# Softmax normalised after the value product, in the sparse attention of a macaron block

## The chip, the core and the metric

The kernel runs on one core of a Trainium2 chip as one program: feed-forward half, sparse attention, feed-forward half. The metric is the device time of one execution in microseconds. The engines are PE (matrix product; PEld is its weight load), DVE (vector), ACT (scalar and activation), POOL (GpSimd) and SP (which here only issues DMAs). Each runs its own instructions in program order and waits on semaphores for the others.

## What is computed

The input is 2 sequences of 1024 tokens of width 128. The change lies in the middle part, where every token attends to 96 keys:

```
_, idx = top_k(I, 96)                      # 64 newest keys, and the 32 best of the older ones
key_c = (c_kv @ W_uk)[bi, idx];  value = (c_kv @ W_uv)[bi, idx]
scores = (q_c . key_c + q_r . key_r) * scale        # 8 heads, content and rotary part
attn = softmax(scores, axis=-1)
out = einsum('bhlk,bhlkd->bhld', attn, value) ... @ W_out
```

The kernel keeps keys and values in the compressed form `c_kv` (32 numbers per token): the scores are taken against `c_kv` and the rotary part, the weights are applied to `c_kv`, and the products with `W_uv` and `W_out` are folded into one matrix used at the end.

## The kernel before

The two feed-forward halves take the first and the last third of the span and are not touched. The attention loop runs over 128 blocks (`NB`) of 16 tokens; a block has 128 rows (4 groups of 4 tokens and 8 heads, so 32 rows per group). Blocks come in 8 phases of 16, and within a phase two "far" and two "near" blocks alternate (`place`). For a block's 16 tokens there are 64-key windows that are local (`KL` for scores; `KVS` or `KV64`, a copy of it shifted by 64 tokens, for values) and 32 selected keys per token.

- A far block's selected rows are gathered by POOL, 4 indirect DMAs a block (line 620), from `kv_rows`, a table in HBM with 128 numbers per token: 64 rotary, 32 of `c_kv`, and 32 ones (`ROWG`; `ROWKV` is the first 96). PE transposes them (line 1001).
- A near block's selected rows come through one-hot matrices: POOL compares the list of indices with key numbers (line 639, 1 to 4 instructions a block, `chunks`), and PE multiplies the one-hot matrices with a table (line 1007). The indices reach POOL's partitions by a store to HBM and a broadcast load on SP (lines 501 and 507), once a phase; the load waits for DVE's last selection step of the phase ahead and for all of the current phase's one-hot matrices.

Per block x the engines then do:

- DVE turns the keys from PSUM with the rotary table into `GTS` (`dve_keys`, 1689); PE forms scores (`pe_scored`, 1020 to 1026); DVE takes the minimum (`dve_least`, 1698); ACT takes the exponential and its row sum `total` (`act_exp`, 1284, followed by a read of the accumulator); DVE takes 1/total (`dve_inverse`, 1703); ACT multiplies the block by it (`act_scaled`, 1290).
- PE transposes the 256 weights of each row (`pe_turned`, 1035), and for near blocks the values too (1038); ACT copies these from PSUM (`act_turned`, 1277); PE applies the weights to the values (`pe_mixed`, 1051 and 1054) and writes 32 rows x 128 columns of bank 7. Four blocks fill 32 rows x 512 columns, and DVE copies them to `OA` (`dve_attended`, two instructions of 256 columns, 1713). Bank 7 holds four such strips.
- Between these, DVE carries out the selection for the phases ahead (`dve_select`, 1647 to 1682) at block numbers fixed by a table, PE its products (982), ACT their relu (1255).

The order is written out by hand. On PE a loop step i is `pe_turned(i)`, `pe_keys(i+3)`, `pe_scored(i+2)`, index products, `pe_mixed(i)`; on DVE it is `dve_inverse(i+1)`, `dve_keys(i+3)`, `dve_least(i+2)`, on every fourth step `dve_attended`, then selection steps. `pe_keys` first calls `pe_stream`, which multiplies an identity by a mask into the bank that the keys will overwrite: 8 matmuls of 512 bf16 columns ahead of a phase's first block, 2 ahead of other far blocks (line 988), 176 in all. Nothing reads their results. After the loop SP moves `OA` to `OAX` by DMA (515) and PE multiplies by the folded matrix (951).

## Time and profile before

| | before |
|---|---|
| median of 3 runs (lowest to highest) | 2060.25 us (2053.6 to 2062.78) |
| the profiled execution | 2060.25 us |
| its span, first to last instruction | 2058.4 us |
| busy over the span: PE, DVE, ACT, POOL | 84%, 62%, 54%, 27% |
| mean granted PE clock over the span; from 790 to 1430 us | 0.849; 0.77 |
| attention loop | about 783 to 1433 us |

The span is the stretch from the first instruction to the last. A busy share is a mean over parts with different limits: POOL is 27% busy over the span and 67% (431.22 of 643 us) from 790 to 1433 us. The granted clock is PE's clock as a share of 2.4 GHz; it takes the values 1.00 and 0.50 (1.2 GHz). "Idle before, releaser" tells how long an engine stood still before an instruction and whose semaphore let it go on.

### The profile page before, as it was taken

To read this page: it belongs to the slowest core of one execution; us is meant where nothing else is said; L and a number is where in the kernel's file an instruction comes from. 1 tells how busy PE (TensorE), PEld (TensorE's weight loads), DVE (VectorE), ACT (ScalarE), POOL (GpSimd) and SP (SyncE) were. 2 spreads that over 40 slices of the span, in tenths; PEclk is the share of its full clock that TensorE was granted. 3 is DMA by queue.
4 is the path that set the end of the run, shared out by engine and by line. 5 is a ranking of instruction groups with operands and counts; after the bars stand their busy time and mean duration, and the time that the engine had idled before them with its cause. 6 is when DMAs were issued, how large, how long until landed. Compare 5 with 4: busy or idle time off the path is not lost.

```text
span 2058.4 us, 34052 instructions
## 1 busy us (share of the span) xinstructions
PE 1719.7 (84%) x10764; PEld 991.9 (48%) x10764; DVE 1285.0 (62%) x3053; ACT 1111.2 (54%) x2328; POOL 548.9 (27%) x479
## 2 busy tenths in 40 slices
PE   3899999699957457888888988888489999969995
PEld 1344444477744114445544545555334444447774
DVE  5677775577785565364655554533467777557777
ACT  3367777388845333333433334333236767738884
POOL 6000000000000505686667866663500000000000
PEclk9699999699987568876967778578769999969998
DMA  4111110111102251111121011120211111002110
GB/s 134 62 50 50 47 46 10 41 67 68 52 10 81 61 119 40 41 32 46 30 62 50 27 43 35 37 61 22 91 62 49 50 49 44 9 29 86 61 52 21
DMA packets 66505, 104.28 MB, mean 51 GB/s; under 512 B 19432, under 2 KB 37296, under 8 KB 63280
## 3 DMA queue, kind: packets, MB, share of 16 engines
q1 hardware_dynamic: 56720, 84.86, 12.9%
q0 software_dynamic: 8192, 16.79, 2.8%
q8 instruction: 73, 1.20, 0.2%
q10 hardware_dynamic: 1456, 0.90, 0.2%
q14 instruction: 64, 0.52, 0.1%
HBM read 74.80 MB, written 8.59 MB: 41 GB/s over the span
## 4 chain that ended last, share of the span: by engine, by line
PE 58%; POOL 11%; issue 10%; DVE 9%; ACT 5%; SPq 3%; DVEq 3%; DMA 1%; ACTq 0%; another core or an unknown queue 0%; POOLq 0%
PE bank L701 10%; PE bank L847 8%; PE bank L685 7%; PE bank L660 6%; PE bank L837 6%; POOL onehot L639 6%; POOL arena L620 5%; PE bank L1007 2%; ACT experts L1152 1%; PE bank L662 1%; PE bank L687 1%; PE bank L1020 1%; DVE arena L1319 1%; SPq L547 1%; PE bank L988 1%
## 5 line engine op out<-in xcount | busy, mean ns | idle before, releaser
L1319 DVE TENSOR_REDUCE arena<-bank 128x1 f32<-128x512 f32 (+3 forms) x768 | 383.1, 551 | 171.4 <-PE bank L662 117.5
L1079 ACT ACTIVATE arena<-bank 128x512 f32<-128x512 f32 (+3 forms) x768 | 335.5, 493 | 145.2 <-PE bank L687 122.2
L566 POOL TENSOR_TENSOR rstd<-vareps,neghalf 128x8 f32<-128x8 f32 x14 | 23.6, 1684 | 1165.3 <-DVE vareps L1312 1165.3
L660 PE MATMUL bank<-arena 72*128 72x512 bf16 (+3 forms) x768 | 259.9, 347 | 39.2 <-DMA arena<-arena 37.1
L620 POOL DMA_INDIRECT arena<-kv_rows,IDX x256 | 251.4, 982 | 153.2 <-ACT IDX L1248 83.9
L685 PE MATMUL bank<-arena 99*128 99x512 bf16 (+3 forms) x768 | 254.7, 335 | 6.1 <-ACT arena L1085 4.3
L639 POOL TENSOR_SCALAR onehot<-XT,const 128x512 fp32r<-128x512 f16 x136 | 212.5, 1574 | 167.3 <-DMA XT<-idx_rows 81.6
L701 PE MATMUL bank<-arena 128*32 128x512 f32 (+3 forms) x1536 | 225.8, 502 | 0.0
L1689 DVE TENSOR_TENSOR HN<-bank,RT 96x512 f32<-96x512 f32 x128 | 87.4, 683 | 218.0 <-PE bank L1007 136.6
L1377 DVE TENSOR_TENSOR experts<-arena,experts 128x512 fp32r<-128x512 f32 x256 | 171.5, 689 | 71.3 <-ACT experts L1152 71.3
L1284 ACT ACTIVATE ATT<-bank,col 128x256 f32<-128x256 f32 x128 | 60.7, 474 | 281.2 <-DVE col L1698 242.9
L1150 ACT ACTIVATE arena<-bank,bias 128x512 f32<-128x512 f32 x256 | 186.0, 727 | 45.8 <-PE bank L837 45.8
L837 PE MATMUL bank<-experts,experts 128*128 128x512 f32 x768 | 196.8, 403 | 7.4 <-ACT experts L1152 5.4
L1152 ACT ACTIVATE experts<-bank,bias 128x512 fp32r<-128x512 f32 x256 | 187.3, 732 | 0.0
L847 PE MATMUL bank<-experts,experts 128*128 128x512 f32 x768 | 182.2, 389 | 0.0
L685 PEld LDWEIGHTS bank<-arena 99*128 99x128 bf16 x768 | 75.5, 98 | 204.9 <-ACT arena L1079 141.0
L1007 PE MATMUL bank<-onehot,tab 128*96 128x512 f32 x272 | 111.2, 523 | 73.2 <-POOL onehot L639 72.3
L837 PEld LDWEIGHTS bank<-experts,experts 128*128 128x128 f32 x768 | 143.7, 192 | 54.7 <-ACT experts L1152 22.3
L847 PEld LDWEIGHTS bank<-experts,experts 128*128 128x128 f32 x768 | 144.1, 188 | 30.4
L660 PEld LDWEIGHTS bank<-arena 72*128 72x128 bf16 x768 | 77.8, 101 | 110.3 <-DVE arena L1319 44.5
L662 PE MATMUL bank<-mask_qk_b,ident_b 128*128 128x128 bf16 x512 | 117.3, 230 | 0.0
L687 PE MATMUL bank<-mask_kq_b,ident_b 128*128 128x128 bf16 x512 | 113.2, 222 | 0.0
(249 smaller groups left out, 2601.7 us busy)
## 6 DMA issues: line engine op xcount, KB each, us to landing
arena<-wt_rows SPq DMA_DIRECT2D x16, 1024.0 KB, 4.7
arena<-q_rows SPq DMA_DIRECT2D x192, 48.0 KB
arena<-k_rows SPq DMA_DIRECT2D x192, 48.0 KB
arena<-in_L_ffn_w SPq DMA_DIRECT2D x32, 256.0 KB, 5.0
arena<-arena SPq DMA_DIRECT2D x32, 256.0 KB
XT<-idx_rows SPq DMA_DIRECT2D x8, 1024.0 KB, 4.7
arena<-kv_rows,IDX POOLq DMA_INDIRECT x256
arena<-HN SPq DMA_DIRECT2D x32, 128.0 KB, 2.4
```

The source lines that it names most:

```text
L620: pool.indirect_dma_start(G[d % GR][:, g, :], None, kv_rows, bass.IndirectOffsetOnAxis(ap=IDX[:, q, k * GB + g:k * GB + g + 1], axis=0))\
L639: pool.tensor_scalar(OH[n % OHR][:, :], IDXB[:, k * BANK:(k + 1) * BANK], cst("key")[:, c:c + 1], None, ALU.is_equal)\
L660: m = pe.matmul(o[:, 0:hi - lo], QB[buf][s][0:ROWS, qt * P:(qt + 1) * P], KB[buf][s][0:ROWS, lo:hi], start=True, stop=True)
L685: m = pe.matmul(o[:, 0:hi - lo], KB[buf][s][0:rows, kc * P:(kc + 1) * P], QB[buf][s][0:rows, lo:hi], start=True, stop=True)
L701: m = pe.matmul(bank[6][r:r + STRIP, lo - hf * BANK:BANK], VS[buf][:, s, kc, :], PT[w % PT_RING][:, 0:(hf + 1) * BANK - lo], start=(kc == ...
L837: m = pe.matmul(bank[f][:, :], W1R[buf][w][:, f * P:(f + 1) * P], XR[x][:, tb * BANK:(tb + 1) * BANK], start=((w, x) == pairs[0]), stop=(( ...
L847: m = pe.matmul(bank[4 + k][:, :], W2R[buf][w][:, f, :], H1R[k][x][:, f, :], start=(f == 0 and (w, x) == pairs[0]), stop=(f == FC - 1 and ...
L1079: act.activation(PT[w % PT_RING][:, 0:m], bank[S_RING + w % S_RING][:, 0:m], ACT.Exp, scale=float(HD) ** -0.5)\
L1150: act.activation(H1[tb % 2][:, f, :], bank[f][:, :], ACT.Gelu_apprx_tanh, bias=bias1[buf][:, f:f + 1])
L1152: act.activation(H1R[tb % 2][0][:, f, :], bank[f][:, :], ACT.Gelu_apprx_tanh, bias=bias1[buf][:, f:f + 1]).then_inc(gelu_done, 1)
L1319: dve.tensor_reduce(rowmax[:, hf, s, qt:qt + 1], bank[u % S_RING][:, 0:n], AX_X, ALU.max).then_inc(max_done, 1)
L1377: dve.tensor_tensor(H1R[tb % 2][1][:, f, :], H1[tb % 2][:, f, :], H1R[tb % 2][0][:, f, :].bitcast(F32), ALU.subtract)\
```

## The change

The row sum is no longer taken by ACT, and the weights are no longer scaled before they are transposed. The block of 32 ones beside `c_kv` is carried along through all steps, so that the value product gives 64 rows: 32 of unnormalised output and 32 that each hold the sum of the weights. After four blocks DVE takes the reciprocal of the 32 x 512 sums and multiplies the output by it while it moves it to `OA`. For this:

- `dve_inverse`, `act_scaled`, the accumulator of `act_exp`, and `pe_stream` with its 176 matmuls go.
- Keys go through PE and DVE with 128 rows in place of 96 (free sizes stay); near values are 64 columns wide per group in place of 32, so ACT's near copy is 512 columns in place of 384; `KV64` is twice as wide, and its six DMAs with it.
- `PB` (weights before the transpose) has 2 buffers in place of 3; bank 7 holds 2 strips in place of 4, so the first value product of group j waits for `dve_attended(j-2)` in place of `(j-4)`.

The declarations of the two semaphores that go are left out here.

```diff
@@ -260,8 +260,6 @@
         col = sb("col", [P, 3])
-        total = sb("total", [P, 3])
-        inverse = sb("inverse", [P, 3])
         best = sb("best", [P, NSEL])
@@ -324,7 +322,7 @@
         KVS = view("sel", (NT, ROWG))
-        KV64 = view("sel", (NT, DC))
+        KV64 = view("sel", (NT, 2 * DC))
         views["sel2"] = views["tab"] = views["sel"]
@@ -349,8 +347,9 @@
         GTS = [HNf[:, i * BANK:(i + 1) * BANK] for i in range(3)]
-        PTS = [ATTf[:, i * 3 * P:(i + 1) * 3 * P] for i in range(2)]
-        PB = [ATTf[:, 6 * P + i * 2 * P:6 * P + (i + 1) * 2 * P] for i in range(3)]
+        RS = HNf[:, 3 * BANK:]
+        PTS = [ATTf[:, i * BANK:(i + 1) * BANK] for i in range(2)]
+        PB = [ATTf[:, 2 * BANK + i * 2 * P:2 * BANK + (i + 1) * 2 * P] for i in range(2)]
         QS = [ATTf[:, 3 * BANK + i * 2 * P:3 * BANK + (i + 1) * 2 * P] for i in range(2)]
@@ -531,9 +529,9 @@
                 t = b * TB
-                sp.dma_start(KV64[0:LW, t + 1:t + TB, :], KVS[LW:P, t:t + TB - 1, 2 * DR:ROWKV]).then_inc(kv64_loaded, 16)
-                sp.dma_start(KV64[LW:P, t:t + TB, :], KVS[0:LW, t:t + TB, 2 * DR:ROWKV]).then_inc(kv64_loaded, 16)
-                sp.dma_start(KV64[0:LW, t, :], KVS[0:LW, t, 2 * DR:ROWKV]).then_inc(kv64_loaded, 16)
+                sp.dma_start(KV64[0:LW, t + 1:t + TB, :], KVS[LW:P, t:t + TB - 1, 2 * DR:]).then_inc(kv64_loaded, 16)
+                sp.dma_start(KV64[LW:P, t:t + TB, :], KVS[0:LW, t:t + TB, 2 * DR:]).then_inc(kv64_loaded, 16)
+                sp.dma_start(KV64[0:LW, t, :], KVS[0:LW, t, 2 * DR:]).then_inc(kv64_loaded, 16)
             sp_near(sp, 0)
@@ -982,29 +980,23 @@
 
-        def pe_stream(pe, o, n):
-
-            for _ in range(n):
-                pe.matmul(o[:, :], ident_b[:, :], maskb[:, 0:2, :].rearrange("p v n -> p (v n)"), start=True, stop=True)
-
         def pe_keys(pe, x):
...
             o = bank[4 + x % 2]
-            pe_stream(pe, o, 8 if x % 16 == 0 else 2 if far else 0)
             if far:
...
                 for g in range(GB):
-                    m = pe.transpose(o[0:ROWKV, g * P:(g + 1) * P], G[d % GR][:, g, 0:ROWKV], ident)
+                    m = pe.transpose(o[:, g * P:(g + 1) * P], G[d % GR][:, g, :], ident)
             else:
...
                     for part in range(2):
-                        m = pe.matmul(o[0:ROWKV, :], TAB[part][:, 4 * b + c, 0:ROWKV], OH[OH_AT[x][c] % OHR][:, :],
+                        m = pe.matmul(o[:, :], TAB[part][:, 4 * b + c, :], OH[OH_AT[x][c] % OHR][:, :],
                                       start=(c == 0 and part == 0), stop=(c == n - 1 and part == 1))
@@ -1028,15 +1020,15 @@
             q, far, tile, k = place(x)
-            pe.wait_ge(pn_ready, x + 1)
+            pe.wait_ge(pb_ready, x + 1)
             if x >= 1:
...
             for part in range(2):
-                m = pe.transpose(bank[6][:, part * P:(part + 1) * P], PB[x % 3][:, part * P:(part + 1) * P], ident)
+                m = pe.transpose(bank[6][:, part * P:(part + 1) * P], PB[x % 2][:, part * P:(part + 1) * P], ident)
             if not far:
                 for g in range(GB):
-                    m = pe.transpose(bank[6][:, 2 * P + g * DC:2 * P + (g + 1) * DC],
-                                     GTS[x % 3][2 * DR:ROWKV, g * P:(g + 1) * P], ident[2 * DR:ROWKV, 2 * DR:ROWKV])
+                    m = pe.transpose(bank[6][:, 2 * P + g * 2 * DC:2 * P + (g + 1) * 2 * DC],
+                                     GTS[x % 3][2 * DR:, g * P:(g + 1) * P], ident[2 * DR:, 2 * DR:])
             m.then_inc(tp_done, 1)
@@ -1044,13 +1036,13 @@
             pe.wait_ge(pts_ready, x + 1)
-            if slot == 0 and j >= 4:
-                pe.wait_ge(oa_ready, j - 3)
-            o = bank[7][j % 4 * DC:(j % 4 + 1) * DC, slot * P:(slot + 1) * P]
+            if slot == 0 and j >= 2:
+                pe.wait_ge(oa_ready, j - 1)
+            o = bank[7][(j % 2) * 2 * DC:(j % 2 + 1) * 2 * DC, slot * P:(slot + 1) * P]
             pts = PTS[x % 2]
-            pe.matmul(o, KVS[:, tile, 2 * DR:ROWKV] if k >= 4 else KV64[:, tile, :], pts[:, 0:P], start=True, stop=True)
+            pe.matmul(o, KVS[:, tile, 2 * DR:] if k >= 4 else KV64[:, tile, :], pts[:, 0:P], start=True, stop=True)
             for g in range(GB):
-                rows = G[(8 * q + k) % GR][:, g, 2 * DR:ROWKV] if far else pts[:, 2 * P + g * DC:2 * P + (g + 1) * DC]
+                rows = G[(8 * q + k) % GR][:, g, 2 * DR:] if far else pts[:, 2 * P + g * 2 * DC:2 * P + (g + 1) * 2 * DC]
                 m = pe.matmul(o[:, g * STRIP:(g + 1) * STRIP], rows, pts[:, P + g * STRIP:P + (g + 1) * STRIP],
@@ -1222,13 +1214,10 @@
                 act_exp(act, x)
-            act_scaled(act, 0)
             for i in range(NB):
...
                     act_queries(act, i // 2 + 2)
-                if i + 1 < NB:
-                    act_scaled(act, i + 1)
                 if i + 2 < NB:
@@ -1273,21 +1262,15 @@
                 act.wait_ge(ob_done, x - 1)
-            n = 2 * P if far else 3 * P
+            n = 2 * P if far else BANK
             act.activation(PTS[x % 2][:, 0:n], bank[6][:, 0:n], ACT.Copy).then_inc(pts_ready, 1)
...
             act.wait_ge(min_ready, x + 1)
-            if x >= 3:
-                act.wait_ge(tp_done, x - 2)
-            act.activation(PB[x % 3], bank[2 + x % 2][:, 0:2 * P], ACT.Exp, scale=-1.0, bias=col[:, x % 3:x % 3 + 1],
-                           accum_out=total[:, x % 3:x % 3 + 1]).then_inc(pb_ready, 1)
-
-        def act_scaled(act, x):
-
-            act.wait_ge(inverse_ready, x + 1)
-            act.activation(PB[x % 3], PB[x % 3], ACT.Identity, scale=inverse[:, x % 3:x % 3 + 1]).then_inc(pn_ready, 1)
+            if x >= 2:
+                act.wait_ge(tp_done, x - 1)
+            act.activation(PB[x % 2], bank[2 + x % 2][:, 0:2 * P], ACT.Exp, scale=-1.0, bias=col[:, x % 3:x % 3 + 1]).then_inc(pb_ready, 1)
 
@@ -1609,10 +1592,7 @@
             dve_least(dve, 1)
-            dve_inverse(dve, 0)
             for i in range(NB):
-                if i + 1 < NB:
-                    dve_inverse(dve, i + 1)
                 if i + 3 < NB:
@@ -1686,9 +1666,8 @@
                 dve.wait_ge(tp_done, x - 2)
-            dve.tensor_tensor(GTS[x % 3][0:ROWKV].rearrange("p (t j) -> p t j", j=NSEL),
-                              bank[4 + x % 2][0:ROWKV, :].rearrange("p (t j) -> p t j", j=NSEL),
-                              RT[0:ROWKV, :].unsqueeze(1).broadcast_to([ROWKV, BT, NSEL]), ALU.mult).then_inc(gts_ready, 1)
+            dve.tensor_tensor(GTS[x % 3].rearrange("p (t j) -> p t j", j=NSEL), bank[4 + x % 2][:, :].rearrange("p (t j) -> p t j", j=NSEL),
+                              RT[:, :].unsqueeze(1).broadcast_to([P, BT, NSEL]), ALU.mult).then_inc(gts_ready, 1)
 
@@ -1697,21 +1676,20 @@
 
-        def dve_inverse(dve, x):
-
-            dve.wait_ge(pb_ready, x + 1)
-            dve.reciprocal(inverse[:, x % 3:x % 3 + 1], total[:, x % 3:x % 3 + 1]).then_inc(inverse_ready, 1)
-
         def dve_attended(dve, j):
...
             dve.wait_ge(ob_done, 4 * j + 4)
-            o = bank[7][j % 4 * DC:(j % 4 + 1) * DC, :]
+            r = (j % 2) * 2 * DC
+            o, inv = bank[7][r:r + DC, :], RS[r:r + DC, :]
+            dve.reciprocal(inv, bank[7][r + DC:r + 2 * DC, :])
+            dve.drain()
             for pair in range(2):
...
                 cols = slice(pair * 2 * P, (pair + 1) * 2 * P)
-                m = dve.tensor_copy(OA[:, :, t0:t0 + 2 * BT].rearrange("p h (g t) -> p g h t", t=4),
-                                    o[:, cols].rearrange("p (g h t) -> p g h t", h=NH, t=4))
+                m = dve.tensor_tensor(OA[:, :, t0:t0 + 2 * BT].rearrange("p h (g t) -> p g h t", t=4),
+                                      o[:, cols].rearrange("p (g h t) -> p g h t", h=NH, t=4),
+                                      inv[:, cols].rearrange("p (g h t) -> p g h t", h=NH, t=4), ALU.mult)
             m.then_inc(oa_ready, 1)
```

On DVE, around a normalisation point near the end of phase 2 (`RT` rows are `dve_keys`, here of block 48; `col` rows `dve_least`, of blocks 46 and 47; `bidh` is the list of near indices of phase 3). Before:

```order
L1698 TENSOR_REDUCE col<-bank 128x1 [waits pb_ready,s_done]
L1713 COPY arena<-bank 32x8x8x4 [waits ob_done]
L1713 COPY arena<-bank 32x8x8x4
L1680 MAX_INDEX bidx<-best,arena 128x8
L1703 RECIPROCAL inverse<-total 128x1 [waits pb_ready]
L1689 TENSOR_TENSOR HN<-bank,RT 96x512 [waits tp_done,gt_done]
L1698 TENSOR_REDUCE col<-bank 128x1 [waits pb_ready,s_done]
L1664 CAST near<-bidx 128x32 [waits idx_stored]
L1666 TENSOR_TENSOR near<-near,const 128x32
L1668 TENSOR_TENSOR bidh<-near,const 128x32
```

The same place in the changed kernel:

```order
L1677 TENSOR_REDUCE col<-bank 128x1 [waits pb_ready,s_done]
L1684 RECIPROCAL HN<-bank 32x512 [waits ob_done]
L1690 TENSOR_TENSOR arena<-bank,HN 32x8x8x4 x2
L1660 MAX_INDEX bidx<-best,arena 128x8
L1669 TENSOR_TENSOR HN<-bank,RT 128x512 [waits tp_done,gt_done]
L1677 TENSOR_REDUCE col<-bank 128x1 [waits pb_ready,s_done]
L1644 CAST near<-bidx 128x32 [waits idx_stored]
L1646 TENSOR_TENSOR near<-near,const 128x32
L1648 TENSOR_TENSOR bidh<-near,const 128x32
```

The 128x1 reciprocals are gone, and a reciprocal of 32 x 512 stands ahead of the keys, the minimum and the index list that follow.

On PE, at the same turn of phases (`pn_ready` is set by `act_scaled`, `pb_ready` by `act_exp`; the 988 rows are the stream, the arena rows of 1001 the keys of block 48). Before:

```order
L1051 MATMUL bank<-ATT,arena 32x128 [waits oa_ready,pts_ready]
L1054 MATMUL bank<-ATT,arena 32x32 x4
L1035 MATMUL bank<-const,ATT 128x128 [waits pts_ready,pn_ready]
L1035 MATMUL bank<-const,ATT 128x128
L988 MATMUL bank<-maskb,ident_b 128x512 [waits gts_ready]
L988 MATMUL bank<-maskb,ident_b 128x512 x7
L1001 MATMUL bank<-const,arena 96x128 [waits gathered0]
L1001 MATMUL bank<-const,arena 96x128 x3
L1020 MATMUL bank<-arena,ATT 128x128 [waits qs_ready,pb_ready]
```

Now:

```order
L1043 MATMUL bank<-ATT,arena 64x128 [waits oa_ready,pts_ready]
L1046 MATMUL bank<-ATT,arena 64x32 x4
L1027 MATMUL bank<-const,ATT 128x128 [waits pts_ready,pb_ready]
L1027 MATMUL bank<-const,ATT 128x128
L993 MATMUL bank<-const,arena 128x128 [waits gathered0,gts_ready]
L993 MATMUL bank<-const,arena 128x128 x3
L1012 MATMUL bank<-arena,ATT 128x128 [waits qs_ready,pb_ready]
```

The eight matmuls between the transposed weights and the keys are gone, and the weights are transposed as soon as the exponential is there.

At the end of the loop DVE has, before (strip 30, the minimum of block 127, strip 31):

```order
L1713 COPY arena<-bank 32x8x8x4 [waits ob_done]
L1713 COPY arena<-bank 32x8x8x4
L1703 RECIPROCAL inverse<-total 128x1 [waits pb_ready]
L1698 TENSOR_REDUCE col<-bank 128x1 [waits pb_ready,s_done]
L1703 RECIPROCAL inverse<-total 128x1 [waits pb_ready]
L1713 COPY arena<-bank 32x8x8x4 [waits ob_done]
L1713 COPY arena<-bank 32x8x8x4
L1628 TENSOR_TENSOR X<-X,bank 128x512 [waits mix_done] x4
```

and now:

```order
L1684 RECIPROCAL HN<-bank 32x512 [waits ob_done]
L1690 TENSOR_TENSOR arena<-bank,HN 32x8x8x4 x2
L1677 TENSOR_REDUCE col<-bank 128x1 [waits pb_ready,s_done]
L1684 RECIPROCAL HN<-bank 32x512 [waits ob_done]
L1690 TENSOR_TENSOR arena<-bank,HN 32x8x8x4 x2
L1608 TENSOR_TENSOR X<-X,bank 128x512 [waits mix_done] x4
```

A wide reciprocal stands ahead of the last block's minimum, and another between the last value product and the strip's move.

## Rows read from the trace of the kernel before

**Rows 1.** Phases 2, 4: length, busy PE, PEld, DVE, ACT, POOL, clock, DMA, GB/s.

```profile
955.00:1029.00 74.00, 63.09 (x506) 37.73 (x505) 43.41 (x106) 31.74 (x90) 49.84 (x44) 0.84 0.13 40
1103.00:1200.00 97.00, 83.90 (x527) 46.74 (x525) 44.46 (x106) 32.40 (x90) 74.52 (x60) 0.72 0.11 34
```

**Rows 2.** POOL in the loop: count | busy us, mean ns | idle before.

```profile
L620 POOL DMA_INDIRECT arena<-kv_rows,IDX x232 | 225.1, 970 | 90.0 <-issue 57.2 <-ACT IDX L1248 27.7 <-PE bank L1007 4.3
L639 POOL TENSOR_SCALAR onehot<-XT,const 128x512 fp32r<-128x512 f16 x132 | 206.3, 1574 | 97.0 <-DMA XT<-idx_rows 81.6 <-PE bank L1007 13.8
```

**Rows 3.** POOL's two long waits there: us in total, times, longest.

```profile
POOL onehot L639 <- DMA XT<-idx_rows: 81.6, 7, 12.9
POOL arena L620 <- ACT IDX L1248: 27.7, 3, 13.2
```

**Rows 4.** Timeline, turn from phase 2 to 3: start, length, instruction [idle <-releaser].

```profile
1019.11 0.76 DVE L1713 COPY arena<-bank 32x256 f32<-32x256 f32 x2
1024.44 0.69 DVE L1689 TENSOR_TENSOR HN<-bank,RT 96x512 f32<-96x512 f32 x1 [4.12 <-PE bank L1001]
1026.46 0.19 DVE L1668 TENSOR_TENSOR bidh<-near,const 128x32 f16<-128x32 f32 x1
1022.03 1.93 PE L988 MATMUL bank<-maskb,ident_b 128*128 128x512 bf16 x8
1033.18 1.57 POOL L639 TENSOR_SCALAR onehot<-XT,const 128x512 fp32r<-128x512 f16 x1 [12.46 <-DMA XT<-idx_rows]
```

**Rows 5.** DVE groups by shape, over the whole span.

```profile
L1703 DVE RECIPROCAL inverse<-total 128x1 f32<-128x1 f32 x128 | 19.2, 150 | 11.9 <-ACT ATT L1284 10.0 <-issue 1.9
L1344 DVE RECIPROCAL arena<-bank 128x8 f32<-128x8 f32 x64 | 8.7, 177 | 39.6 <-PE bank L710 39.6
L1457 DVE RECIPROCAL g<-g 128x16 f32<-128x16 f32 x2 | 0.5, 253 | 0.1
L1713 DVE COPY arena<-bank 32x256 f32<-32x256 f32 x64 | 24.1, 412 | 4.4 <-PE bank L1054 3.7
```

**Rows 6.** Three stretches of the loop without a wait for POOL, all engines.

```profile
797.00:824.00 27.00, 26.04 (x238) 16.48 (x239) 22.05 (x48) 13.15 (x36) 19.16 (x15) 1.00 0.04 13
978.00:1006.00 28.00, 25.84 (x256) 16.66 (x255) 22.43 (x57) 13.55 (x44) 20.50 (x18) 1.00 0.11 32
1301.00:1343.00 42.00, 42.00 (x245) 25.27 (x244) 25.86 (x57) 14.78 (x45) 24.46 (x23) 0.50 0.08 24
```

**Rows 7.** The same, line L1026 alone (one instruction a block): PE, PEld.

```profile
978.00:1006.00 28.00, 2.54 (x9) 0.86 (x9) 1.00 0.11 32
1301.00:1343.00 42.00, 3.15 (x8) 0.82 (x8) 0.50 0.08 24
```

**Rows 8.** PE's timeline where the loop begins.

```profile
783.30 3.49 PE L988 MATMUL bank<-maskb,ident_b 128*128 128x512 bf16 x8 [11.42 <-DVE tab L1602]
```

**Rows 9.** Timeline of the loop's end: DVE, PE, SP.

```profile
1426.39 0.76 DVE L1713 COPY arena<-bank 32x256 f32<-32x256 f32 x2
1427.87 0.42 DVE L1698 TENSOR_REDUCE col<-bank 128x1 f32<-128x256 f32 x1 [0.66 <-PE bank L1026]
1430.33 0.44 PE L1035 MATMUL bank<-const,ATT 128*128 128x128 f32 x2
1432.81 0.77 DVE L1713 COPY arena<-bank 32x256 f32<-32x256 f32 x2 [3.71 <-PE bank L1054]
1433.60 10.04 SPq L515 DMA_DIRECT2D arena<-arena  x16
1444.85 1.43 PE L951 MATMUL bank<-MO,arena 128*128 128x128 f32 x5 [7.18 <-DMA arena<-arena]
```

**Rows 10.** Weight loads 96 and 128 columns wide: ns min/median/max.

```profile
L1001 PEld LDWEIGHTS bank<-const,arena x12: 126/127/128, 991.3 to 1004.4; 128*96 128x96 f32 x12
L1035 PEld LDWEIGHTS bank<-const,ATT x12: 138/141/144, 990.3 to 1006.8; 128*128 128x128 f32 x12
```

**Rows 11.** The stream's matmuls, line 988, in the loop.

```profile
L988 PE MATMUL bank<-maskb,ident_b 128*128 128x512 bf16 x166 | 57.4, 455 | 0.0
```

More of the change, by code:

```diff
@@ L406, in build @@
         gt_done, gts_ready, s_done, min_ready, pb_ready = (sem(n) for n in ("gt_done", "gts_ready", "s_done", "min_ready", "pb_ready"))
-        inverse_ready, pn_ready = sem("inverse_ready"), sem("pn_ready")
         tp_done, pts_ready, ob_done, oa_ready = (sem(n) for n in ("tp_done", "pts_ready", "ob_done", "oa_ready"))
```

## The prediction

> **What bounds the kernel now.** I read the page's engine shares first, then busy time by stretch, then the waits, then timelines at the places where an engine stands still. Only the attention loop is changed, some 650 of 2058 us, so the question is what sets its pace.
>
> The loop has two paces. POOL's is the first: 232 gathers at 970 ns with some 0.3 us between them and 132 one-hots at 1574 ns [rows 2]. In phase 4, whose near blocks take 28 one-hots, POOL is busy 74.52 of 97 us, and with its gaps and one long wait it is never free; in phase 2, with 12 one-hots, it is busy only 49.84 of 74 [rows 1]. POOL's long waits are seven for the broadcast index list, 81.6 us in total, and three for the far indices, 27.7 us [rows 3]. They are not spent on the transfer alone. At the turn to phase 3, POOL stood 12.46 us until 1033.18, but the index list was written only at 1026.46 [rows 4], so about half of that wait is PE and DVE getting through their blocks.
>
> The second pace is that of PE and DVE together where POOL is ahead. From 978 to 1006 us PE is busy 25.84 of 28 us at clock 1.00 and DVE 22.43; from 797 to 824 it is 26.04 and 22.05 of 27 [rows 6]. From 1301 to 1343 PE is busy all 42 us at clock 0.50 while 8 blocks pass, 5.2 us each, against 3.1 us a block at clock 1.00 [rows 6, 7]. DVE is thus the second engine at the full clock, at 80%, and has room only at the low clock.
>
> **The change part by part.**
>
> *The wide reciprocal.* It is the largest new term, and the trace has none of its size. DVE reciprocals of 1, 8 and 16 elements take 150, 177 and 253 ns [rows 5]: from 8 to 16 elements 76 ns for 8, or 9.5 ns each; from 1 to 16, 103 ns for 15, or 6.9. The copy of 256 columns takes 412 ns [rows 5], so an ordinary operation costs about 1 ns an element. For 512 elements: lower end 0.7 us (an ordinary operation), 3.7 us by the smaller slope (253 + 496 x 6.9), 5.0 us by the larger. I take 4.4, between the two slopes, since the reciprocal rows themselves are nearest. The Trainium skill, in "VectorE: DVE Perf Modes", section "First, the fixed hardware budget", says that DVE divides iteratively with a repeat count of 8; an estimate from that and DVE's 0.96 GHz is 4.3 us, and the trace's slopes agree with it in size.
>
> 32 times 4.4 is 141 us more on DVE; gone are 128 small reciprocals of 150 ns, 19.2 us [rows 5]. The multiply that replaces the copy has the same 256 columns and I leave it at 0.41 us. Per block that is +1.1 - 0.15 = +0.95 us of DVE.
>
> - Where DVE and PE set the pace: 978 to 1006 holds 9 blocks, so DVE's load becomes 22.43 + 8.6 = 31.0 us in a stretch of 28; 797 to 824, 8 blocks, 22.05 + 7.6 = 29.7 in 27 [rows 6, 7]. At perfect packing that is +3.0 and +2.7 us. DVE is not packed perfectly: it now stands 5 to 5.6 us in each; if half stays, +5.8 and +5.2. I take +4.5 each, two more such stretches (phases 3 and 7) at half of it, and 1 us each in phases 1 and 5, where PE later waits for one-hots anyway: **+15.5 us** (0 if POOL hides it all, 30 at the worst). In phases 4 and 6 (POOL's pace; low clock, DVE 25.86 of 42) nothing.
> - At the seven turns: before, DVE ends its copy at 1019.87 and then stands 4.12 us until PE has the next keys at 1024.44; PE spends 1.93 us of that on eight stream matmuls [rows 4]. After, PE is there 1.9 us earlier, but DVE comes from the reciprocal at 1019.11 + 4.4 + 0.8 = 1024.3, plus a selection step of 0.3: 1024.6. The gain of the stream is eaten, the turn moves by +0.15: 7 times, **+1 us**. With a reciprocal of 0.7 us it would be -1.9 each, -13.
> - At the end it is on the path with no cover. DVE's minimum of block 127 starts at 1427.87, and its copy before that at 1426.39 [rows 9]; with the reciprocal the minimum starts at 1426.39 + 5.2 = 1431.6, and the transpose of block 127, now at 1430.33, follows the exponential at about 1432.4: +2. After the last value product the copy at 1432.81 releases SP's 16 DMAs at 1433.60, and PE waits for them until 1444.85 [rows 9]; 4.4 us go in between. **+6.5 us**.
>
> *The stream goes.* 166 matmuls in the window cover 57.4 us of PE [rows 11], 0.24 us each at the full clock (1.93 for eight [rows 4]) and 0.43 at the low one (3.49 for eight [rows 8]). What it gives: at the loop's start 3.49 us end, but the third block needs three one-hots from POOL, 4.7 us, so **-1.5** (0 to -3.5). From 1301 to 1343 four far blocks lose 0.86 us each, 3.4 us; in the other low and full stretches some 2 us more are on the path: **-5.5**. At the full clock 0.48 us per far block would be gained, but DVE is the later engine there.
>
> *Wider weights.* PE's weight loads of 128 columns take 141 ns against 127 for 96 [rows 10], so the four key loads cost +0.06 us; the value products' eight loads go from 32 to 64 columns, at most the same step each. Up to +0.15 us a block, on the path in some 20 blocks: **+3**.
>
> *ACT* loses a scaling and an accumulator read per block and gains 128 columns in 64 copies. It sits in no stretch at the limit (14.78 of 42, 13.55 of 28 [rows 6]), and the scaling of block i+1 runs a step before its transpose. 0, from -3 (short last blocks) to 0. *Two strips in place of four, two PB buffers*: the strip j-2 is moved four steps before its place is needed, over 12 us, against 5.2 us for the new move; the exponential's wait for an earlier transpose comes behind an ACT copy that waited for the same. 0 both. *KV64*: the same descriptors with 256 bytes for 128, ahead of the placing of the queries; 0, at most +1.
>
> *The clock.* The granted clock is 0.77 on average over the loop, at 0.50 in phases' slower stretches and at 1.00 in others [rows 1, 6]. The stream keeps PE at work ahead of far blocks; without it, and with PE held back by DVE, more blocks may fall into the low level. The trace does not show how many. One end is 0. The other is all of some 30 blocks that now run at 1.00 off POOL's pace: each (5.2 - 3.1 - 0.5 for the stream that is gone) = 1.6 us, 48 us, of which DVE's 15 are then hidden. I take 7 blocks, **+11 us**. The Trainium skill ("TensorE: Matmul & The Clock Gate", section "HAM oscillation — how this bites in real kernels") puts a low clock down to gaps in PE's work. The trace only half agrees: from 1301 to 1343 PE has no gap and stays at 0.50 [rows 6]. By the page the clock term would be only what DVE's delays open as gaps; by the row a PE without gaps is no safeguard, and the term can be larger.
>
> **Sum.** 15.5 + 1 + 6.5 - 1.5 - 5.5 + 3 + 11 = +30. The profiled execution took 2060.25 us, with a span of 2058.4; it is also the median of the three. Forecast 2090 us, +1.5%.
>
> **The rivals.**
>
> 1. *The clock stays low through the loop.* For: half of the loop is already low, and DVE's delays open gaps on PE. Against: the clock has come back in every phase so far, and each of those rises would have to be owed to the stream. Price: 48 (DVE's 15 hidden) + 6.5 + 1 - 1.5 - 5.5 + 3 = +51 over stretches that POOL does not pace: 2111 us.
> 2. *POOL's pace hides all but the ends.* For: 67% busy plus waits. Against: PE and DVE decide half of POOL's waits. +6.5 + 1 - 1.5 - 3 = +3: 2063 us.
> 3. *The other side: the reciprocal costs like any 512-column operation.* It decides from about 2 us downwards, where the turns gain. At 0.7 us: turns -13, start -1.5, stream -5.5, end +1, wider weights +3, DVE unchanged: -16, 2044 us. Against: three reciprocal rows rise with size far faster than a copy.
>
> **How the numbers follow.** Forecast (2070 to 2103) 0.46, rival 1 0.20, rival 2 0.19, rival 3 0.15. About 0.5%, 10 us, is what a measurement tells from no change. Faster: 0.13 (rival 3 but for 0.02). Same: 0.17 of rival 2, 0.03 of the forecast's low end and 0.02 of rival 3, 0.21. Slower: 0.66. The range 2054 to 2120 leaves out most of rival 3 and the far end of rival 1, about 0.18; the forecast's own is 2070 to 2103.
>
> **What would show it.** DVE's reciprocal of 32 x 512 near 4.4 us, 32 of them; below 2 us the forecast's main term falls. DVE busy some 120 us more over the loop, and above 90% in the stretches off POOL's pace. At the turns, POOL's wait for the index list still near 12 us and keys held up by DVE, not PE. From the last value product to the last SP issue 5 us more. The mean clock over the loop at 0.70 to 0.75 in place of 0.77; at 0.6 rival 1 holds, and at 0.8 the clock term was wrong in sign. The forecast is wrong if phases 2 and 3, 74 us each, get shorter.

## The result and the profile after

| | before | after |
|---|---|---|
| median of 4 runs (lowest to highest) | 2061.10 us (2053.60 to 2062.78) | 2115.59 us (2113.15 to 2126.50) |
| ratio after/before, 95% interval | | 1.031 [1.0273, 1.0348] |
| the profiled execution, its span | 2060.25, 2058.4 us | 2128.80, 2127.0 us |
| mean granted clock over the span | 0.849 | 0.801 |

The changed kernel is 3.1% slower: 54.5 us, against +30 in the forecast. The time is inside the range, the sign was right, and the size was off by almost half. The profiled execution of after is slower than its median, so its trace overstates the loss by some 13 us; a second trace of the same kernel is used below beside it. The ratios here and below leave out executions in a slower state of the chip, of which e2 and g3 further down had one each; their medians are over all executions.

**The loop as a whole.** The profile by stretches, here the attention loop. The columns are the stretch, its length, then the busy time and number of instructions of PE, PEld, DVE, ACT and POOL, the granted clock, the DMA share and GB/s.

```profile
790.00:1490.00 700.00, 629.50 (x3807) 411.85 (x3808) 415.02 (x690) 186.10 (x438) 430.65 (x364) 0.65 0.12 36
```

Before, the same part ran from 790 to about 1430 us with DVE at about 328, POOL at 431 and the clock at 0.77. POOL has the same work, so what POOL alone paces hasn't changed. DVE has 87 us more, where the forecast had 120. PE has some 75 us more, although 57.4 us of stream matmuls are gone [rows 11]: that is the first sign of a term that the sum lacked. It has two possible causes, work that got longer or a lower clock, and the clock did fall, to 0.65.

**The reciprocal.** Instructions on the tile `HN`, with minimum, median and maximum in ns and the first and last start. The first row is the new reciprocal, the second its multiply.

```profile
L1684 DVE RECIPROCAL HN<-bank x32: 3348/3356/3364, 808.1 to 1499.0; 32x512 f32<-32x512 f32 x32
L1690 DVE TENSOR_TENSOR arena<-bank,HN x64: 401/411/419, 811.5 to 1502.8; 32x256 f32<-32x256 f32 x64
```

3.36 us, or 6.55 ns an element, where the sum had 4.4. The slope from 1 to 16 elements, 6.9 ns [rows 5], would have been the better choice of the two. The multiply costs what the copy did.

**Weight loads of the value product.** Two lines at the same clock of 0.50, from 1420 to 1462 us, minimum, median and maximum as above: L1043 is the local part of `pe_mixed`, L1046 the selected part.

```profile
L1043 PEld LDWEIGHTS bank<-ATT,arena x16: 182/206/231, 1421.0 to 1457.3; 128*64 128x64 f32 x16
L1046 PEld LDWEIGHTS bank<-ATT x32: 227/227/231, 1421.2 to 1458.3; 128*64 128x64 f32 x32
L1046 PE MATMUL bank<-ATT x32: 261/294/296, 1421.4 to 1458.4; 128*64 128x32 f32 x32
```

A selected value product has only 32 columns to stream, and its weight load of 64 columns takes 227 ns. There are 8 such loads and 2 local ones a block. What they took with 32 columns is shown with the experiment on them.

**Who waits.** The waits of POOL, from 785 to 1500 us: total, times, longest.

```profile
POOL onehot L637 <- DMA XT<-idx_rows: 90.9, 7, 19.3
POOL arena L618 <- ACT IDX L1237: 45.0, 3, 18.6
POOL onehot L637 <- PE bank L999: 33.6, 8, 7.4
```

The first two were 81.6 and 27.7 us before [rows 3]. The third was 13.8 us [rows 2]. All three hang on work that PE and DVE do in earlier blocks, so a slower block comes back as a longer wait of POOL: POOL didn't hide the loss, it passed it on. Not every wait grew. For the index list of phases 1 and 2 POOL stood 10.67 and 9.84 us (12.45 and 11.86 before), for that of phases 3 and 4 it stood 17.95 and 19.33 us (12.46 and 10.11 before).

**The turn from phase 2 to 3**, timeline, start and length in us. It answers to [rows 4].

```profile
1037.13 3.35 DVE L1684 RECIPROCAL HN<-bank 32x512 f32<-32x512 f32 x1
1038.70 0.60 PE L993 MATMUL bank<-const,arena 128*128 128x128 f32 x4
1041.95 0.67 DVE L1669 TENSOR_TENSOR HN<-bank,RT 128x512 f32<-128x512 f32 x1
1043.57 0.19 DVE L1648 TENSOR_TENSOR bidh<-near,const 128x32 f16<-128x32 f32 x1
1049.85 1.57 POOL L637 TENSOR_SCALAR onehot<-XT,const 128x512 fp32r<-128x512 f16 x1 [17.95 <-DMA XT<-idx_rows]
```

PE has the next keys ready at 1039.30, but DVE comes to them only at 1041.95, from the reciprocal. That is the forecast's picture of a turn: before, DVE waited for PE here, now the keys wait for DVE. The turn itself is shorter, though: from the first instruction that moves the strip to the index list it takes 6.44 us (1037.13 to 1043.57), against 7.35 before (1019.11 to 1026.46 [rows 4]). POOL's wait, 12.46 us before [rows 4], is 17.95; from the index list to POOL's start it is 6.3 us in after and 6.7 before, so the increase lies wholly ahead of the list.

**The loop's end**, timeline; it answers to [rows 9].

```profile
1491.67 0.40 DVE L1677 TENSOR_REDUCE col<-bank 128x1 f32<-128x256 f32 x1
1495.52 0.69 PE L1027 MATMUL bank<-const,ATT 128*128 128x128 f32 x2
1497.99 1.01 PE L1046 MATMUL bank<-ATT 128*64 128x32 f32 x8
1499.04 3.36 DVE L1684 RECIPROCAL HN<-bank 32x512 f32<-32x512 f32 x1 [6.97 <-PE bank L1046]
1502.48 0.76 DVE L1690 TENSOR_TENSOR arena<-bank,HN 32x256 f32<-32x256 f32 x2
1503.26 10.04 SPq L513 DMA_DIRECT2D arena<-arena  x16
1514.52 5.72 PE L949 MATMUL bank<-MO,arena 128*128 128x128 f32 x26 [9.90 <-DMA arena<-arena]
```

The reciprocal stands with no cover between the last product and SP's DMAs: 3.4 us for the forecast's 4.4. The first two rows are the minimum of block 127 and the transposes of its weights, which begin 3.5 us after that minimum has ended. At the low clock PE is still at block 126 then, so the 2 us that the forecast adds for a late minimum are not there.

### The profile page after: what moved, and what is told of

It is laid out like the page before. It is cut to its first block, busy times and chain, and to the rows that moved or that the text cites. A ratio compares the mean times of both kernels' runs of the same rounds, so it can differ in the third digit from the quotient of the medians.

```text
span 2127.0 us, 33446 instructions
## 1 busy us (share of the span) xinstructions
PE 1800.0 (85%) x10588; PEld 1085.1 (51%) x10588; DVE 1378.9 (65%) x2957; ACT 1050.6 (49%) x2072; POOL 549.1 (26%) x479
## 4 chain that ended last, share of the span: by engine, by line
PE 61%; issue 10%; POOL 9%; DVE 8%; ACT 4%; DVEq 3%; SPq 2%; DMA 1%; ACTq 0%; POOLq 0%; another core or an unknown queue 0%
PE bank L699 10%; PE bank L845 8%; PE bank L683 7%; PE bank L658 6%; PE bank L835 5%; POOL onehot L637 5%; POOL arena L618 4%; PE bank L999 3%; PE bank L1046 2%; PE bank L1012 2%; PE bank L1027 2%; PE bank L1043 2%; PE bank L1015 2%; ACT experts L1144 2%; PE bank L660 1%
## 5 line engine op out<-in xcount | busy, mean ns | idle before, releaser
L1669 DVE TENSOR_TENSOR HN<-bank,RT 128x512 f32<-128x512 f32 x128 | 87.9, 687 | 207.1 <-PE bank L999 164.3
L999 PE MATMUL bank<-onehot,tab 128*128 128x512 f32 x272 | 129.0, 602 | 48.6 <-POOL onehot L637 48.4
```

The lines of the kernel that those rows point to most:

```text
L999: m = pe.matmul(o[:, :], TAB[part][:, 4 * b + c, :], OH[OH_AT[x][c] % OHR][:, :], start=(c == 0 and part == 0), stop=(c == n - 1 and part ...
```

## The experiments

Each ratio is to the kernel before on the same chip, with its 95% interval. The kernel before ran at 2055.31 us in the first group (e1 to e4), 2039.23 in the second (f1 to f4) and 2054.47 in the third (g1 to g4), so times are compared within a group and ratios across groups with care. The first and the third group ran on one chip, the second on another. A ratio is the estimate on record and not the quotient of two medians; the two differ by up to 0.3%.

| run | what it is | us | ratio |
|---|---|---|---|
| e1 | after, stream put back | 2133.34 | 1.0349 [1.0259, 1.0438] |
| e2 | before, stream gone | 2050.12 | 0.9994 [0.9955, 1.0034] |
| e3 | after, copy for the reciprocal | 2104.81 | 1.0212 [1.0148, 1.0276] |
| e4 | e1 and e3 together | 2099.27 | 1.0183 [1.0114, 1.0251] |
| f1 | after, keys 96 rows | 2127.10 | 1.0426 [1.0392, 1.0460] |
| f2 | f1, and near values transposed 32 wide | 2132.81 | 1.0445 [1.0409, 1.0482] |
| f3 | after, value products 32 wide | 2090.43 | 1.0239 [1.0198, 1.0279] |
| f4 | before, all widths as in after | 2109.63 | 1.0329 [1.0285, 1.0374] |
| g1 | after, unchanged | 2124.09 | 1.0347 [1.0314, 1.0379] |
| g2 | e2 with the wide reciprocal alone | 2091.32 | 1.0174 [1.0141, 1.0207] |
| g3 | e2 with the widths alone | 2109.85 | 1.0272 [1.0235, 1.0309] |
| g4 | before, only the 8-matmul streams gone | 2045.37 | 0.9959 [0.9935, 0.9983] |

### Is it the stream, and the clock through it?

The theories on record were that DVE's reciprocal (D) or a clock that falls without the stream (C) makes the loss, against wider weights (W). e1 and e2 put the stream back and take it away alone.

```diff
# e1, in pe_keys of after (pe_stream as before)
+            pe_stream(pe, o, 8 if x % 16 == 0 else 2 if far else 0)
# e2, in pe_keys of before
-            pe_stream(pe, o, 8 if x % 16 == 0 else 2 if far else 0)
```

> The changed kernel with the stream of identity matmuls put back as it was (8 ahead of a phase's first block, 2 ahead of other far blocks). Theory C (the clock: most of the loss beyond the forecast is that without the stream the granted clock of the loop fell from 0.77 to 0.65): the clock comes back to 0.75 or more and the time falls to 2080 to 2095 us, the rest being the wide reciprocal. Theory D (the reciprocal: DVE's 107 us hold PE back, and the clock falls as a consequence of that): the clock stays near 0.67 and the time at 2105 us or more. Theory W (wider weight loads slow PE): time stays at 2115 us or above, since the stream adds work.

> The kernel before with the stream taken out and nothing else. Theory C: the loop's clock falls to about 0.65 and the time rises to 2085 to 2105 us. Theory D: nothing holds PE back, so the clock stays at 0.75 and the time falls by the stream's length on the path, to 2045 to 2058 us. Theory W: as D.

Measured: e2 makes no difference that shows, 0.9994, and e1 is not faster than after: 1.0349, where after has 1.031 and 1.0347 (g1). Theory C is refuted by both. The profile by stretches of e2, over its loop up to the last block and over four blocks (49 to 53) at the low clock:

```profile
790.00:1413.92 623.92, 540.30 (x3832) 323.31 (x3832) 328.89 (x790) 247.16 (x692) 433.51 (x365) 0.71 0.14 40
1043.45:1063.94 20.49, 18.29 (x117) 11.01 (x113) 11.78 (x28) 6.21 (x18) 16.93 (x16) 0.50 0.26 65
```

The clock did fall without the stream, from 0.77 to 0.71, and yet the loop isn't longer: PE's busy time is 540 us, not above the 552 that it had with the stream. What the lower clock costs is about what 57.4 us of matmuls without use cost. So the stream bought clock and paid for it, and its removal is no part of the loss, to within the 0.4% of e2's interval.

### Is it the reciprocal?

e3 puts a copy in the place of the reciprocal, and e4 does so with the stream there. The division is left out of both.

```diff
# e3, in dve_attended of after (e4: the same on e1)
-            dve.reciprocal(inv, bank[7][r + DC:r + 2 * DC, :])
+            dve.tensor_copy(inv, bank[7][r + DC:r + 2 * DC, :])
```

> The changed kernel with a copy of the 32 x 512 sums in place of their reciprocal, so the division by the sum is left out and DVE loses about 2.7 us in every fourth block, 85 us in all. Theory C: the stream is still missing, so the clock stays under 0.70 and the time at 2090 us or more. Theory D: clock back to 0.75 and time 2050 to 2065 us. Theory W: 2095 to 2110 us.

> Both at once: the changed kernel with the stream back and with a copy in place of the reciprocal (the division by the sum is left out). What is left of the change is the wider weights, ACT's lighter work and the smaller rings. Theories C and D: 2055 to 2065 us, as before. Theory W: 2075 us or more, and slower than before by more than the sum can owe to anything else.

Measured: 1.0212 and 1.0183. Without the reciprocal, the loss is still 2%, and DVE's busy time is nearly that of before. The profile by stretches of e3, its loop and eight blocks (113 to 121) at the low clock; the last row is that of the copies:

```profile
790.00:1478.92 688.92, 638.09 (x3821) 413.58 (x3820) 339.38 (x693) 189.37 (x438) 432.17 (x364) 0.63 0.13 36
1409.17:1450.88 41.71, 40.00 (x228) 26.75 (x225) 11.81 (x22) 8.94 (x20) 28.42 (x25) 0.50 0.17 45
```

```profile
L1684 DVE COPY HN<-bank x32: 681/689/697, 809.4 to 1487.6; 32x512 f32<-32x512 f32 x32
```

The same eight blocks of after, with the reciprocal:

```profile
1420.64:1462.33 41.69, 39.99 (x228) 26.73 (x225) 16.86 (x22) 8.94 (x20) 28.45 (x25) 0.50 0.16 45
```

DVE has 11.81 us of work in one and 16.86 in the other, and both stretches take 41.7 us. In this stretch, at the low clock, DVE's extra work is covered by PE. Where the loop begins the clock is full, and there it is not: blocks 3 to 9, with the first two reciprocals, take 28.60 us in after, 23.81 before and 23.46 in e3. The three rows in this order:

```profile
796.04:824.64 28.60, 25.60 (x199) 17.54 (x195) 21.69 (x37) 8.83 (x20) 19.69 (x17) 0.88 0.07 19
```

```profile
800.08:823.89 23.81, 22.85 (x205) 14.38 (x201) 19.68 (x43) 12.16 (x33) 16.09 (x13) 1.00 0.05 15
```

```profile
797.40:820.86 23.46, 22.95 (x199) 15.63 (x195) 19.91 (x37) 8.86 (x20) 16.77 (x14) 1.00 0.06 15
```

Part of the difference is the clock, which is 0.88 here in after and 1.00 in the other two.

With DVE hardly loaded, PE's 638 us must come from PE's own work or clock: here theory D fell too (it put e3 at 2050 to 2065 us), and the widths, the one large part still untouched, were next.

### Which width?

f1 takes the 32 extra rows out of the key and one-hot products (the ones are set once in `HN` instead), f2 also out of the near values' transposes, and f3 takes only the value products back to 32 columns. f3 has no sums; its reciprocal reads the output rows, so DVE's load stays. f4 is the other way round: all widths, two strips and the wide `KV64` in the kernel before, with its stream and its normalisation. Only the lines that matter are shown.

```diff
# f1 (in both key branches)
-                    m = pe.transpose(o[:, g * P:(g + 1) * P], G[d % GR][:, g, :], ident)
+                    m = pe.transpose(o[0:ROWKV, g * P:(g + 1) * P], G[d % GR][:, g, 0:ROWKV], ident)
+            dve.memset(HNf[ROWKV:, 0:3 * BANK], 1.0)
# f3, pe_mixed
-            pe.matmul(o, KVS[:, tile, 2 * DR:] if k >= 4 else KV64[:, tile, :], pts[:, 0:P], start=True, stop=True)
+            pe.matmul(o, KVS[:, tile, 2 * DR:ROWKV] if k >= 4 else KV64[:, tile, 0:DC], pts[:, 0:P], start=True, stop=True)
-                rows = G[(8 * q + k) % GR][:, g, 2 * DR:] if far else pts[:, 2 * P + g * 2 * DC:2 * P + (g + 1) * 2 * DC]
+                rows = G[(8 * q + k) % GR][:, g, 2 * DR:ROWKV] if far else pts[:, 2 * P + g * 2 * DC:2 * P + g * 2 * DC + DC]
# f4, pe_mixed of before (keys, near values, KV64 and strips widened as in after)
-                rows = G[(8 * q + k) % GR][:, g, 2 * DR:ROWKV] if far else pts[:, 2 * P + g * DC:2 * P + (g + 1) * DC]
+                rows = G[(8 * q + k) % GR][:, g, 2 * DR:] if far else pts[:, 2 * P + g * 2 * DC:2 * P + (g + 1) * 2 * DC]
```

> The changed kernel, but keys and one-hot products go through PE and DVE with 96 rows as before; the 32 rows of ones in the key buffers are written once ahead of the loop. Theory W1 (the wider weight loads slow PE in every block, and most of it is the value product's eight loads per block, 32 to 64 columns): only 4 key loads or 2 to 8 table loads a block get shorter, the far block at the low clock falls from 5.33 to about 5.1 us and the time by 3 to 12 us against the changed kernel, 2105 to 2112 us on a chip where that takes 2116. Theory W2 (the keys' 96 to 128 is what counts): falls by 20 us or more. Theory N (width costs nothing, rings or other order does it): within 3 us of the changed kernel.

> As the kernel with narrow keys, and the near values are transposed and copied 32 columns wide per group, with the ones preset in ACT's two buffers (ACT then copies in two instructions). W1: another 0 to 4 us less in near blocks, since the moving side grows by 32 columns only, 2103 to 2110 us. W2: no further change. N: no change, or 2 to 4 us more by ACT's second instruction.

> The changed kernel with only the value product back at 32 weight columns; the sums are left out, and DVE takes the reciprocal of the output rows themselves so that its load is unchanged (the outputs are not normalised). W1: this takes away most of the width's cost: near and far blocks at the low clock fall from 4.53 and 5.33 us to about 4.2 and 5.0, the time by 20 to 35 us, to 2080 to 2095. W2: under 8 us. N: under 3 us.

> The kernel before with the widths of the change alone: keys of 128 rows, near values and value products of 64 columns, two strips in bank 7, KV64 doubled; row sums, small reciprocals, ACT's scaling and the stream as before, and no wide reciprocal. W1 and W2: 2085 to 2100 us, that is the larger part of the change's loss without any change in how the softmax is normalised, blocks at the low clock longer by 0.4 to 0.5 us. N: 2055 to 2065 us.

Measured: f1 and f2 gain nothing that shows (after itself did not run in this group, so that the 3 to 12 us expected of f1 can't be told by time), f3 gains 37 us on f1, and some 15 to 22 us on after by its ratios in the other groups (1.031 and 1.0347). f4 is 70 us above the kernel before, 1.0329, where f1, which has the wide products and the reciprocal, is 88 us above it. That is most of the loss without any change of the normalisation, and more than the 2085 to 2100 us that were expected of f4. The same eight blocks of f1 and f3:

```profile
1421.72:1463.25 41.53, 39.78 (x228) 26.10 (x225) 16.82 (x22) 8.95 (x20) 28.37 (x25) 0.50 0.17 45
```

```profile
1396.75:1435.45 38.70, 36.58 (x229) 22.74 (x225) 16.75 (x22) 8.93 (x20) 28.39 (x25) 0.50 0.18 49
L1043 PEld LDWEIGHTS bank<-ATT,arena x16: 128/141/154, 1397.1 to 1430.8; 128*32 128x32 f32 x16
L1046 PEld LDWEIGHTS bank<-ATT x32: 157/157/178, 1397.3 to 1431.5; 128*32 128x32 f32 x32
L1046 PE MATMUL bank<-ATT x32: 241/241/261, 1397.5 to 1431.6; 128*32 128x32 f32 x32
```

Clock, DVE, ACT and POOL are the same as in after. The stretch is 2.99 us shorter (41.69 to 38.70), PEld's busy time 3.99 us. A load of the selected part falls from 227 to 157 ns, one of the local part from 206 to 141: 8 x 70 + 2 x 65 = 0.69 us of load records a block. The records overlap one another, so that PEld's busy time falls by 0.50 a block, and 2.99 / 8 = **0.37 us a block** is on the path. f1's widths are worth 0.16 us in eight blocks, 0.02 a block. At the full clock the same comparison is, for blocks 3 to 7, of after and then of f3:

```profile
796.04:810.63 14.59, 14.42 (x129) 9.83 (x125) 12.81 (x20) 5.21 (x12) 8.95 (x8) 1.00 0.05 15
```

```profile
798.00:811.94 13.94, 13.57 (x129) 8.97 (x125) 12.64 (x20) 5.00 (x12) 8.47 (x8) 1.00 0.05 15
```

0.65 us in four blocks, 0.16 a block. The loads of the same stretches, after's first:

```profile
L1046 PEld LDWEIGHTS bank<-ATT x16: 137/138/138, 799.5 to 804.1; 128*64 128x64 f32 x16
```

```profile
L1046 PEld LDWEIGHTS bank<-ATT x16: 110/113/113, 801.3 to 805.5; 128*32 128x32 f32 x16
```

So the step from 32 to 64 columns is 25 ns at the full clock and 70 at the low one. [Rows 10], on which the forecast's price rested, were read where the clock was 1.00.

### One part at a time, on one chip

g1 repeats after; g2 and g3 add one part each to the kernel without the stream, which e2 showed to be no different from before. g2 leaves out the sums: its reciprocal reads the output rows. g4 tries the one edit that the trace speaks for, to drop the eight matmuls at the turns and to keep the pairs.

```diff
# g2: f1's and f3's narrow products in after, near values and ACT's copy 32 wide again, and
-            dve.reciprocal(inv, bank[7][r + DC:r + 2 * DC, :])
+            dve.reciprocal(inv, o)
# g3: f4 without the stream
-            pe_stream(pe, o, 8 if x % 16 == 0 else 2 if far else 0)
# g4: before
-            pe_stream(pe, o, 8 if x % 16 == 0 else 2 if far else 0)
+            pe_stream(pe, o, 2 if far and x % 16 else 0)
```

> The changed kernel as it is, so that it stands beside the others on one chip. Width theory and reciprocal theory alike: 1.03 to 1.045 of the kernel before.

> The changed kernel with every width back (96-row keys, 32-column near values and value products); the wide reciprocal stays and is taken of the output rows themselves, the sums are left out. What is left of the change is the wide reciprocal, the missing stream, and ACT's lighter work. Width theory (the value product's weights carry most of the loss): 1.010 to 1.022 of before, blocks at the low clock at 4.10 and 4.83 us. Reciprocal theory (its 107 us on DVE carry most of it): 1.03 or more, as the changed kernel.

> The kernel before with the widths and without the stream, normalised as before. Width theory: 1.02 to 1.035, as with the stream, since the stream did not matter in the narrow kernel either. Clock theory in a weaker form (the stream matters only where PE sets the pace, as it does with wide weights): 1.045 or more. Reciprocal theory: 1.01 or less.

> The kernel before with only the eight stream matmuls at each phase's first block taken out; the twos stay. They stand at the turn of phases, where POOL waits for the next index list: 1.93 us at the full clock at seven turns and up to 3.5 us at the start. If they do nothing for the clock that follows, 0.992 to 0.997 of before; if they hold it up, 1.00 or more.

Measured: the widths alone cost 55 us (g3), the reciprocal alone 37 (g2), both 70 (g1) and not 92. All three lie where the width theory put them, and g4 lies in the range of a stream that does nothing for the clock. The loops of the three by stretches, g3, g2, g1, each up to its last block:

```profile
790.00:1465.20 675.20, 614.75 (x3833) 399.85 (x3833) 327.97 (x790) 254.81 (x692) 433.33 (x365) 0.67 0.13 37
```

```profile
790.00:1454.23 664.23, 572.86 (x3832) 344.02 (x3830) 412.50 (x692) 178.99 (x438) 433.20 (x365) 0.67 0.13 38
```

```profile
790.00:1479.31 689.31, 612.50 (x3832) 399.63 (x3833) 415.63 (x692) 185.69 (x438) 432.77 (x366) 0.68 0.12 36
```

Against e2's 623.92 us these are +51, +40 and +65. Part of each comes by way of the clock. It knows two levels, so a mean of m means (1 - m) x 2 of the time at 0.50: before 0.46 of 638 us, 293 us; e2 0.58 of 624, 362; g3 446, g2 438, g1 441. With either part alone, some 80 us more of the loop run at the low level than in e2. For g3 the direct price can be estimated: 128 blocks at 0.37 us are 47 us; with 446 us at the low level in blocks of about 5.2, some 86 blocks at 0.37 and 42 at 0.16 are 39. The rest of the 51 us, between 4 and 12, is a rough estimate of what came through the clock, since some blocks pay more than 0.37 and others nothing. After itself shows the same from its two traces: the first had 0.65 and 700 us, the second 0.68 and 689.

That most blocks do pay shows block by block, from one start of the mask's product (L1018 of after) to the next. 48 blocks ran at 0.50 (for 97% of their time or more) in g1 and in g2 alike, and 39 of them are longer in g1 by more than 0.1 us, most by 0.43 to 0.53; of 33 that ran at 1.00 in both, 25 are, most by 0.21 to 0.26. POOL's share doesn't hide it either. The stretch of e2 above, blocks 49 to 53, took 20.49 us; in g3 it takes 21.88:

```profile
1041.99:1063.87 21.88, 20.17 (x115) 13.49 (x113) 10.87 (x26) 5.94 (x16) 18.34 (x18) 0.50 0.25 65
```

That the sum isn't reached with both parts fits e3's stretch: where PE's blocks are longer and the clock is low, the reciprocal is covered. Where the clock is full, it isn't. Between g1 and g3, which have the same widths, 50 of 52 blocks that ran at 0.50 in both agree in length within 0.05 us; of 30 that ran at 1.00 in both, seven are 0.76 to 1.82 us longer in g1. Timeline of after at full clock:

```profile
1299.97 3.36 DVE L1684 RECIPROCAL HN<-bank 32x512 f32<-32x512 f32 x1
1303.41 0.76 DVE L1690 TENSOR_TENSOR arena<-bank,HN 32x256 f32<-32x256 f32 x2
1303.56 0.66 PE L993 MATMUL bank<-const,arena 128*128 128x128 f32 x4
1305.12 0.69 DVE L1669 TENSOR_TENSOR HN<-bank,RT 128x512 f32<-128x512 f32 x1
1305.87 0.42 PE L1015 MATMUL bank<-HN,ATT 96*32 96x128 f32 x8 [1.23 <-DVE HN L1669]
```

PE's transposes of the keys end at 1304.22; DVE, late from the reciprocal and with two selection steps still ahead of the keys, turns them at 1305.12, and PE stands 1.23 us.

g4 is 0.9959 [0.9935, 0.9983], 0.4% below before, the only kernel here whose interval lies below 1. It is a small gain, seen on one chip, and e2's interval, from 0.9955, takes it in, so it is not shown that keeping the pairs is better than taking the whole stream out.

## Why the prediction was right in sign and wrong in size

- **The step that failed is "Wider weights", +3 us.** It priced the step from 32 to 64 columns by that from 96 to 128, 127 to 141 ns [rows 10], "at most the same step each. Up to +0.15 us a block, on the path in some 20 blocks". Both factors were too small. The loads of the value product grew by 65 to 70 ns each at the low clock and by 25 at the full one, not by 14, which gives 0.37 and 0.16 us a block: the step was larger than that of [rows 10] even at their clock, and these rows were all taken at the full clock for a loop that is half of its time at the low one; and they are on the path in most blocks (39 of the 48 and 25 of the 33 above), not in 20, because where POOL waits, it waits for what PE and DVE did before. There are also ten such loads a block, where the sum counted eight. Alone, this part measured 2.7% (g3) to 3.3% (f4), 55 to 70 us; on top of the reciprocal 33 us (g1 less g2).
- **The wide reciprocal, 15.5 + 1 + 6.5 = 23 us.** One takes 3.36 us, not 4.4. The estimate of 4.3 us that the prediction set beside it is as far off. Alone it costs 37 us (g2), on top of the widths 14 (g1 less g3, two kernels with the same widths and no stream), 19 (g1 less e3) or 34 (e1 less e4, with wide intervals); the forecast lies among these. The mechanism holds at the full clock (1305.87) and at the end (3.4 us, without the 2 that were added ahead of it); at the low clock it costs nothing (e3's 41.71 against 41.69). At the turn the keys do wait for DVE (1041.95), but with 3.36 us in the sum's own arithmetic they come 0.9 us earlier than before, not 0.15 later, and this turn did get 0.9 us shorter; the one from phase 6 to 7 went from 5.28 to 6.08 us. In the first stretch that the sum named, blocks 3 to 9 hold the first two reciprocals, and their loss was as forecast there: 28.60 us in after and 23.81 before, 4.8 us for +4.5.
- **The stream goes, -1.5 - 5.5, and the clock term, +11.** These two belong together and their sum, +4, was near the truth, +0 (e2). But the reason given was only half right: the clock fell without the stream to 0.71, and the further fall to between 0.63 and 0.68 came with either of the two other parts, stream or no stream (f4, with it, has a mean of 0.827 over its span against 0.849 of before in the profiles).
- **Rival 1, clock low through the loop, 2111 us.** It named a time near the one measured, and in phases 2, 3 and 7 after's clock had a mean of 0.58, 0.56 and 0.50. Its mechanism, that the rises were owed to the stream, is refuted by e2; 0.65 is also short of the 0.50 that it supposed. The time was right by luck, for another reason. Its price also rests on a misreading: "3.1 us a block" at the full clock divides 28 us by the nine starts of L1026 in it, while from start to start blocks 36 to 44 took 26.90 us, 3.36 each. The price of a low block is then 1.3 us and not 1.6, and the rival's time some 8 us lower.
- **Rival 2, POOL hides it,** is refuted: POOL's two index waits grew by 9.3 and 17.3 us. **Rival 3, a cheap reciprocal,** is refuted by 3356 ns. In the chances the parts named for "same" add up to 0.22, not 0.21, and those for "slower" to 0.65.
- **ACT, strips, KV64 at 0.** f1 and f2 bear out that the other widths cost nothing that shows; the two strips and the wide `KV64` were not tried apart from the rest.
- **Open:** why the clock stays low longer when PE has more work, and with it how much of the 54.5 us came through the clock. In the last 8 blocks (119 to 127) e2 runs at the full level and takes 20.86 us; e1, with as little idle time on PE and the stream present, runs at the low one and takes 41.21:

```profile
1393.06:1413.92 20.86, 20.81 (x224) 13.79 (x220) 10.66 (x28) 11.71 (x35) 5.36 (x4) 1.00 0.03 8
```

```profile
1460.65:1501.86 41.21, 41.21 (x230) 26.85 (x227) 16.75 (x23) 8.62 (x19) 5.61 (x4) 0.50 0.02 4
```

PE is busy all the time in both. The clock thus can't be read from PE's busy share alone, and no run here says what decides it. The Trainium skill ("TensorE: Matmul & The Clock Gate", section "HAM oscillation — how this bites in real kernels") puts a low clock down to gaps in PE's work. In e1 PE did stand 2.20 us, until 1456.99, before the level fell, but e1's row does not agree that gaps keep it low: 41 us without one did not bring the full level back.

## What to carry to other kernels

Extra columns that ride along in a matrix product are not free when the matrix that grows is the stationary one and the moving one is short: compare the duration of the weight load with that of its matmul in the trace, and price the new width at each clock level that the part runs at, and by a step of the same size. Before a cost is counted "in 20 blocks only", ask what the engine that seems to hide it waits for. And two parts that slow different engines do not add: measure each alone and both together.

## What the runs showed of the hardware

- An fp32 weight load under short matmuls (32 columns) takes 157 ns for 32 columns and 227 for 64 at the clock of 0.50, 113 and 138 ns at 1.00. At 0.50 the keys' load of 128 columns (L993), under matmuls of 128 columns, takes 230 ns, hardly more than the 227 of one of 64. The first row is after's, the second f1's with 96 columns, 201 ns. The price does not grow in proportion to the columns, and a step of 32 columns does not cost the same everywhere.

```profile
L993 PEld LDWEIGHTS bank<-const,arena x16: 183/230/230, 1429.2 to 1455.0; 128*128 128x128 f32 x16
```

```profile
L993 PEld LDWEIGHTS bank<-const,arena x16: 157/201/203, 1430.3 to 1456.0; 128*96 128x96 f32 x16
```

- DVE's reciprocal of 512 elements takes 3.36 us, five times a copy of the same size (0.69 us), 6.55 ns an element.
- 57.4 us of matmuls that keep PE busy raised the loop's mean clock from 0.71 to 0.77 and changed the time by nothing that can be told from zero (0.9994 [0.9955, 1.0034]).
- One kernel's loop took 700 us in one trace and 689 in another, at a mean clock of 0.65 and 0.68.
